# A mixture-of-experts stage computed on each token's two chosen experts, with rows sorted by expert through DRAM

## What is computed

```python
def _L1_ffn_ref(x, Wr, Wg, Wu, Wd):
    probs = jax.nn.softmax(x @ Wr, axis=-1)
    topk_w, topk_idx = jax.lax.top_k(probs, K)          # K = 2, E = 8
    topk_w = topk_w / jnp.sum(topk_w, axis=-1, keepdims=True)
    output = jnp.zeros_like(x)
    for i in range(E):
        sel = topk_idx == i
        w_i = jnp.sum(topk_w * sel.astype(x.dtype), axis=-1, keepdims=True)
        h = jax.nn.silu(x @ Wg[i]) * (x @ Wu[i])        # 256 x 256 each
        e_out = h @ Wd[i]
        output = output + w_i * e_out
    return output
...
    x = x + _L1_ffn_ref(_layernorm(x, axis=-1), L1_ffn_Wr, L1_ffn_Wg, L1_ffn_Wu, L1_ffn_Wd)
```

## Time and profile before

| | us |
|---|---|
| three runs | 3267.83, 3267.85, 3267.93 |
| median | 3267.85 |
| span of the profiled execution, first to last instruction | 3263.3 |
| median less span | 4.55 |
| of the span: expert stage, 2553.8 to 3263.3 | 709.5 |

### The profile page before, as it was taken

One profiled execution on the slowest core, in us unless ns is written; L12 is line 12 of the kernel. 1 busy time (PEld: TensorE's weight loads), 2 busy tenths in 40 slices (PEclk: granted clock), 3 DMA queues, 4 the chain that ended last, 5 costly groups with the idle time before them and its releaser, 6 DMA issues. The chain is left out here.

```text
span 3263.3 us, 78862 instructions
## 1 busy us (share of the span) xinstructions
PE 2803.0 (86%) x26196; PEld 1987.6 (61%) x26196; DVE 2373.2 (73%) x6843; ACT 1129.7 (35%) x2570; POOL 916.8 (28%) x1406
## 2 busy tenths in 40 slices
PE   3545549999999659998888849999999999999999
PEld 2433325555555359996666624444444799999999
DVE  6999967777777766666999947787777455555555
ACT  1222224555555422222333315565555211111111
POOL 3444432222222246664444422222222000000000
PEclk8676669999999879999999959999999999999999
DMA  3000033444444100000000044444444000000000
GB/s 88 0 0 0 0 97 84 87 86 86 86 86 85 24 1 0 0 0 1 0 0 0 0 128 92 94 87 94 94 85 84 5 5 6 6 6 5 6 6 7
DMA packets 230889, 132.42 MB, mean 41 GB/s; under 512 B 31328, under 2 KB 230400, under 8 KB 230816
## 3 DMA queue, kind: packets, MB, share of 16 engines
q1 hardware_dynamic: 226016, 127.05, 18.6%
...
## 5 line engine op out<-in xcount | busy, mean ns | idle before, releaser
L723 ACT ACTIVATE xattn_pr<-ps 128x384 f32<-128x384 f32 (+1 forms) x1024 | 536.6, 543 | 506.4 <-PE ps L493 233.3
L597 DVE TENSOR_REDUCE xattn_mx<-ps 128x2 f32<-128x512 f32 x512 | 342.0, 679 | 138.9 <-PE ps L459 128.7
L472 PE MATMUL ps<-xattn_qp,xattn_kp 128*128 128x192 bf16 (+1 forms) x2048 | 416.0, 264 | 3.0 <-DMA xattn_qp<-xattn_mrow 2.7
L459 PE MATMUL ps<-xattn_kp,xattn_qp 96*128 96x192 bf16 (+1 forms) x2048 | 372.5, 264 | 47.9 <-DMA xattn_kp<-xattn_rows 42.3
L593 DVE CUSTOM_DVE_ANT_0 xattn_masked<-ps,xattn_band 128x192 bf16<-128x192 f32 x1024 | 323.9, 353 | 106.9 <-issue 46.5
L472 PEld LDWEIGHTS ps<-xattn_qp,xattn_kp 128*128 128x128 bf16 x2048 | 163.9, 98 | 283.4 <-ACT xattn_pr L723 143.5
L1057 DVE SCALAR_TENSOR_TENSOR moe_tg<-moe_tanh,ps 128x256 f32<-128x256 f32 x256 | 107.8, 421 | 287.4 <-ACT moe_tanh L1027 287.4
L493 PE MATMUL ps<-xattn_pr,xattn_vs 128*32 128x256 f32 (+1 forms) x4096 | 303.3, 368 | 0.0
L493 PE MATMUL ps<-xattn_pr,xattn_ones 128*32 128x256 f32 (+1 forms) x4096 | 303.2, 368 | 0.0
L1027 ACT ACTIVATE moe_tanh<-ps 128x256 f32<-128x256 f32 x256 | 98.1, 383 | 587.1 <-PE ps L956 587.1
L956 PE MATMUL ps<-moe_xt,expert_g 128*128 128x128 f32 x2048 | 274.4, 277 | 0.0
...
## 6 DMA issues: line engine op xcount, KB each, us to landing
xattn_rows<-xattn_parts SPq DMA_DIRECT2D x128, 192.0 KB, 2.1
xattn_qp<-xattn_rows SPq DMA_DIRECT2D x256, 96.0 KB, 3.2
xattn_kp<-xattn_rows SPq DMA_DIRECT2D x256, 96.0 KB, 3.7
xattn_rows<-xattn_parts SPq DMA_DIRECT2D x128, 128.0 KB, 2.1
xattn_rows<-xattn_parts SPq DMA_DIRECT2D x128, 64.0 KB, 1.8
...
xattn_ctx<-in_ctx SPq DMA_DIRECT2D x32, 128.0 KB, 3.9
```

Of the source, the lines that this page charges most:

```text
L459: mm = nc.tensor.matmul(ps[:, BANK_S + j % RING, mt * D:mt * D + width], qp[u][s][0:R_MAX, h, mt * P:(mt + 1) * P], kp[u][s][0:R_MAX, h, l ...
L472: mm = nc.tensor.matmul(out, kp[u][s][:, h, nt * P:(nt + 1) * P], qp[u][s][:, h, lo:lo + width], start=True, stop=not banded)
L597: ins = nc.vector.tensor_reduce(mx[s][:, h * NT:(h + 1) * NT], ps[:, BANK_S + j % RING, :].rearrange("p (m n) -> p m n", m=NT), AX.X, ALU.max)
L723: nc.scalar.activation(out, src, ACT.Exp, scale=HD ** -0.5).then_inc(exped, 1)
```

## The change

The expert stage `gated_mlp(... moe ...)` is replaced by `routed_experts`, and its loops are written out.

- **Routing first.** All 32 pairs are normalised into `xn`, transposed and multiplied by the router. The steps of the softmax and of the ranks are done for groups of eight pairs (`G = 8`), four groups. PE counts, by products with a triangular matrix and with ones (`places`, `count`), which place each token has among those of its expert; DVE makes from it the row of each token in a table sorted by expert (`choices`, `block_table`), one table for each half of the tokens (`PARTS_R = 2`, 16 pairs each). Each expert's rows begin on a multiple of 128, so a half has 39 blocks of 128 rows at most, `BLOCKS = 2 * 2048 / 128 + 7`, and 39 are computed always.
- **Rows sorted through DRAM.** POOL scatters the normalised rows by indirect transfers, one per pair and choice: 32 per half, each of 128 rows of 1 KB. Rows of the table that no token uses stay zero from `clear_regions`, a new block of ten stores by SP at the start of the RWKV stage.
- **Blocks.** For each of the 78 blocks SP loads the rows (`load_block`, four buffers), PE transposes them, multiplies them by gate and up of the block's one expert in one product of 512 columns per weight tile (now the rows are the stationary side), transposes the hidden rows and multiplies by down. The number of the expert is read from SBUF into a register of PE (`expert_of`), and the weights are addressed by it. ACT copies both transposes out of PSUM and takes the tanh; DVE makes the hidden rows and copies the result to SBUF, SP stores it to DRAM.
- **Rows brought back.** POOL gathers for each pair the rows of both choices (`gather`, 64 in all, three buffers for each choice), DVE adds them by weight to `core.x` (`add_up`), SP stores. The sums of the first half are laid between the blocks of the second, those of the second half follow its last block.

The diff, cut to the parts that the working below speaks of:

```diff
--- before.py
+++ after.py
+PARTS_R = 2
+REGION = SEQS * T // PARTS_R
+BLOCKS = 2 * REGION // P + E8 - 1
...
-    g, u, d = (core.sb(f"expert_{n}", [P, NT, E8, D], ctx=ctx) for n in "gud")
+    gu = core.sb("expert_gu", [P, NT, E8, 2 * D], ctx=ctx)
+    down = core.sb("expert_d", [P, NT, E8, D], ctx=ctx)
...
+    each = 8
+    zero = core.sb("region_zero", [P, each, D], ctx=ctx)
+    made, cleared = nc.alloc_semaphore(name="region_zero_made"), nc.alloc_semaphore(name="region_cleared")
+    starts = range(0, ROWS, P * each)
+            nc.gpsimd.memset(zero[:].rearrange("p a d -> p (a d)"), 0.0).then_inc(made, 1)
+        @block.sync
+        def _(sp):
+            sp.wait_ge(made, 1)
+            for x in x_in:
+                for at in starts:
+                    n = min(each, (ROWS - at) // P)
+                    to = x[at:at + n * P, :].rearrange("(p a) d -> p a d", a=n)
+                    sp.dma_start(to, zero[:, 0:n, :]).then_inc(cleared, 16)
...
+        def sums_after(part, b):
+            if part == 0:
+                return []
+            return range(PP * b // BLOCKS, PP * (b + 1) // BLOCKS)
...
+                def load_block(part, b):
+                    n = idx(part, b)
+                    if b == 0:
+                        sp.wait_ge(scattered[part], 2 * 16 * PP)
+                    wait(sp, xb_turned, n - RB + 1)
+                    sp.dma_start(xb[n % RB][:], x_in[part][b * P:(b + 1) * P, :]).then_inc(xb_in[n % RB], 16)
+                def store_block(part, b):
+                    n = idx(part, b)
+                    sp.wait_ge(y_kept, n + 1)
+                    sp.dma_start(y_out[part][b * P:(b + 1) * P, :], yb[n % RB][:]).then_inc(yb_left[n % RB], 16)
+                def store_out(p):
+                    sp.wait_ge(summed, 2 * (p + 1))
+                    sp.dma_start(out_dram.rearrange("(n s) t d -> n (s t) d", s=S2)[p], acc[p % 2][:]).then_inc(left[p % 2], 16)
+                for b in range(RB - 1):
+                    load_block(0, b)
+                for n, (part, b) in enumerate(blocks()):
+                    if n + RB - 1 < PARTS_R * BLOCKS:
+                        load_block(*divmod(n + RB - 1, BLOCKS))
+                    store_block(part, b)
+                    for p in sums_after(part, b):
+                        store_out(p)
+                for p in range(PAIRS - PP, PAIRS):
+                    store_out(p)
...
+                def places(g):
+                    pe.wait_ge(routed, ROUTED * g + 11)
+                    wait(pe, routed, ROUTED * g)
+                    if g % PER == 0:
+                        wait(pe, tabled, TABLE * (g // PER - 1) + 1)
+                    flat = lambda q: sel[:, q, :, :].rearrange("p i e -> p (i e)")
+                    nc.tensor.matmul(ps[:, BANK_P, 0:G * E8], c[:, C_BEFORE:C_BEFORE + P], flat(g), start=True, stop=False)
+                    ones = c[:, C_ONES:C_ONES + P]
+                    for q in range(g // PER * PER, g):
+                        for i in range(G):
+                            nc.tensor.matmul(ps[:, BANK_P, 0:G * E8].rearrange("p (i e) -> p i e", e=E8), ones,
+                                             sel[:, q, i:i + 1, :].broadcast_to([P, G, E8]), start=False, stop=False)
+                    for i in range(G - 1):
+                        mm = nc.tensor.matmul(ps[:, BANK_P, (i + 1) * E8:G * E8].rearrange("p (i e) -> p i e", e=E8), ones,
+                                              sel[:, g, i:i + 1, :].broadcast_to([P, G - 1 - i, E8]), start=False, stop=(i == G - 2))
+                    mm.then_inc(placed, 1)
+                def count(part):
+                    last = (part + 1) * PER - 1
+                    pe.wait_ge(routed, ROUTED * (last + 1))
+                    n = 0
+                    for q in range(part * PER, last + 1):
+                        for i in range(G):
+                            n += 1
+                            mm = nc.tensor.matmul(ps[:, BANK_P, 0:E8], c[:, C_ONES:C_ONES + P], sel[:, q, i, :], start=(n == 1), stop=(n == PP))
+                    mm.then_inc(counted, 1)
...
+                def gate_up(part, b, e):
+                    n = idx(part, b)
+                    pe.wait_ge(xb_kept, n + 1)
+                    wait(pe, hidden, 2 * (n - 1))
+                    for kt in range(NT):
+                        mm = nc.tensor.matmul(ps[:, BANK_G + n % 2, :], xbt[n % 2][:, kt, :], gu[:, kt, bass.ds(e, 1), :].rearrange("p a f -> p (a f)"),
+                                              start=(kt == 0), stop=(kt == NT - 1))
+                    mm.then_inc(gu_made, 1)
+                def expert_of(n):
+                    part, b = divmod(n, BLOCKS)
+                    if b == 0:
+                        pe.wait_ge(tabled, TABLE * part + 9)
+                    return pe.value_load(expert[part][0:1, b:b + 1], min_val=0, max_val=E8 - 1)
+                turn_x(0)
+                pe.wait_ge(*landed)
+                for p in range(PAIRS):
+                    if p + 1 < PAIRS:
+                        turn_x(p + 1)
+                    logit_product(p)
+                    if p % G == G - 1:
+                        places(p // G)
+                        if p // G % PER == PER - 1:
+                            count(p // G // PER)
+                N = PARTS_R * BLOCKS
+                e = {0: expert_of(0)}
+                turn_block(0, 0)
+                gate_up(0, 0, e[0])
+                e[1] = expert_of(1)
+                turn_block(0, 1)
+                for n in range(N):
+                    if n + 2 < N:
+                        e[n + 2] = expert_of(n + 2)
+                    if n + 1 < N:
+                        gate_up(*divmod(n + 1, BLOCKS), e[n + 1])
+                    turn_hidden(*divmod(n, BLOCKS))
+                    if n + 2 < N:
+                        turn_block(*divmod(n + 2, BLOCKS))
+                    down_product(*divmod(n, BLOCKS), e[n])
...
+                keep_block(0, 0)
+                tanh(0, 0)
+                keep_block(0, 1)
+                for n in range(N):
+                    if n + 1 < N:
+                        tanh(*divmod(n + 1, BLOCKS))
+                    keep_hidden(*divmod(n, BLOCKS))
+                    if n + 2 < N:
+                        keep_block(*divmod(n + 2, BLOCKS))
...
+                for p in range(G):
+                    normalise_x(p)
+                for g in range(GROUPS):
+                    for p in range((g + 1) * G, min((g + 2) * G, PAIRS)):
+                        normalise_x(p)
+                    probabilities(g)
+                    ranks(g)
+                    choices(g)
+                    if g % PER == PER - 1:
+                        block_table(g // PER)
+                N = PARTS_R * BLOCKS
+                make_hidden(0, 0)
+                for n, (part, b) in enumerate(blocks()):
+                    if n + 1 < N:
+                        make_hidden(*divmod(n + 1, BLOCKS))
+                    keep_y(part, b)
+                    for p in sums_after(part, b):
+                        add_up(p)
+                for p in range(PAIRS - PP, PAIRS):
+                    add_up(p)
...
+                def scatter(p):
+                    for k in range(2):
+                        g.indirect_dma_start(x_in[p // PP], bass.IndirectOffsetOnAxis(ap=at[k][:, p:p + 1], axis=0), xn[:, p, :], None,
+                                             ).then_inc(scattered[p // PP], 16)
+                def gather(p):
+                    r = p % RY
+                    if p % PP == 0:
+                        for q in range(RB):
+                            g.wait_ge(yb_left[q], 16 * uses((p // PP + 1) * BLOCKS, q, RB))
+                    for k, y in enumerate((y1, y2)):
+                        wait(g, summed, 2 * (p - RY) + k + 1)
+                        g.indirect_dma_start(y[r][:], None, y_out[p // PP], bass.IndirectOffsetOnAxis(ap=at[k][:, p:p + 1], axis=0),
+                                             ).then_inc(y_in[k][r], 16)
+                for part in range(PARTS_R):
+                    g.wait_ge(tabled, TABLE * (part + 1))
+                    for p in range(part * PP, (part + 1) * PP):
+                        scatter(p)
+                for p in range(PAIRS):
+                    gather(p)
...
-        time_mixing(core, "rwkv", rwkv, mu, decay[:], bonus)
+        with ExitStack() as stage:
+            regions, cleared = clear_regions(core, stage)
+            time_mixing(core, "rwkv", rwkv, mu, decay[:], bonus)
+            nc.sync.wait_ge(*cleared)
...
-            gated_mlp(core, "moe", E8, lambda j, kt, ft: g[:, kt, j, ft * P:(ft + 1) * P],
-                      lambda j, kt, ft: u[:, kt, j, ft * P:(ft + 1) * P], lambda j, ft: d[:, ft, j, :], r, out, landed)
+            routed_experts(core, "moe", experts, regions, out, landed)
```

297 lines of the change are left out of this document (291 added, 6 removed).

## The result

| | before | after |
|---|---|---|
| median of four runs, us | 3267.84 | 3060.64 (3058.24 to 3063.06) |
| ratio to before | | 0.9366, 95% interval 0.9353 to 0.9379 |
| profiled execution, its time and span | see ahead | 3063.06 and 3060.9 |
| start of the expert stage, us from the span's start | 2553.8 | 2552.5 |
| length of the stage | 709.5 | 508.4 |

The change gains 207.2 us; 265.8 were forecast. The time lies in the range, 58.6 us above the forecast. The gain is in the expert stage, as its length shows (201.1 us shorter); what the stages ahead of it lost and won nearly cancels. In the combined kernel, the last experiment, one execution of four took 7128.8 us, which nothing here explains: the median in the table counts it, the median of the other three is 2969.28, and the interval of the ratio is that of those three.

What follows compares the result with a forecast made beforehand. PE was taken to bound the expert stage of 709.5 us. Start 2553.8, insertion 8, head 96, blocks 289 and tail 51 gave 2997.8; with 4.55 between span and median, 3002 us, range 2925 to 3120.

Steps and rivals of the forecast that it cites:

- G, the price of an indirect transfer: POOL's time for one scatter or gather: 1.3 us, twice a plain transfer, bounded between 0.64 and 5.9.
- the tail: After the last block: second half's gathers, additions and last store, together 51 us, 30 at the cheapest transfer price.
- the slower rival: POOL waits for each indirect transfer to land; from 4.5 us each all 128 are exposed, 3361 us at 5.7; chance 0.04.
- the first rival: Indirect transfers on POOL cost 2 to 4 us, lengthening head and tail: 3048 to 3176 us; chance 0.14.
- The chain of a block: Each of 78 blocks: gate and up, draining, hops, ACT's tanh and copy, down; 3.60 us, 3.7 with register operation.
- its register term: On PE in each block: register operation before each waiting product 0.09 us; loading the expert's number nothing, hidden behind down.
- The head: Routing before the first block: 96 us (70 to 130), from 98 by POOL's scatters and 68 to 107 by PE.
- Second half's scatters are hidden: 32 scatters on POOL, 42 us, run beside 39 blocks of 144 us and cost nothing.
- The insertion: Clearing the table before the RWKV stage, with its barrier: fill 2 to 4 us, ten issues 5.1; 8 us (6 to 10).
- a register load that is exposed: In the blocks, loading the expert's number costs up to 0.8 us each: 3067 us; chance 0.14 shared with late block loads.
- The lock of DVE and POOL: In the head, first 32 scatters and DVE's routing exclude one another; first block 35 us later, 3037 us; chance 0.12.
- The low clock: PE's clock stays low through the blocks: 6.4 us a block, 211 us more, 3213 us; chance 0.04.

Runs made afterwards that it cites:

- the combined kernel: Changed kernel with second half's scatters spread, hidden transposes after down, register load moved before the remaining wait, clearing without stage boundary; 2971.37 us, ratio 0.9076 to 0.9113.
- e7_load_moved: Changed kernel with the register load of the expert's number moved from before gate and up to before down; 2989.22 us, ratio 0.9137 to 0.9167.
- the narrow scatters: Changed kernel with every scatter moving only the first 32 of a row's 256 numbers; 3000.60 us, ratio 0.9166 to 0.9202.

## Why the prediction came out as it did

The profiled execution took 3063.06 us against 3002: 61 us, point by point.

- **G, the price of an indirect transfer: right.** Forecast 1.3 us, measured 0.96 us busy and 1.27 apart for scatters, 0.95 and 1.25 for gathers. This carried most of the risk, and the tail with it: forecast 51, measured 50.8. POOL waits for no landing, so the slower rival falls; so does the first rival. The Trainium skill, "GPSIMD Engine Reference", "Performance pitfalls for Q7 kernels", has a cost for a kernel that reads each gather index by a command of its own (some 102 cycles), from which the estimate of 10.9 us for 128 indices was worked out; the trace doesn't bear it out for this instruction, which reads 128 indices and is done in 0.96 us.
- **The chain of a block: right, and its register term too small.** The chain was put at 3.60 and is 3.59 with fixed experts. What was mis-sized is "one register operation ahead of each waiting product costs about 0.09" together with a load at nothing: with the register the period is 3.83, so 0.24 in place of 0.09, and 0.13 over the forecast's 3.70, 10 us in 77 blocks. The load was taken as hidden beneath the down product; moving it beneath PE's wait for ACT won 0.15 of these, and the 0.08 that stays with the products is what was forecast for the register operations. The term that was wrong is the load's own nothing. The Trainium skill, "DMA: Bandwidth & Descriptors", "Latency and other measured facts", gives such a load a floor of about 600 ns. The trace agrees, a little below it: 0.56 us where nothing covers it.
- **The pipeline's first block: left out.** Multiplying 78 blocks by the period leaves out that the first takes 10.0 us from its transposes to its copy (2675.2 to 2685.2), 6 more than a period.
- **The head: right where there is no hole.** Forecast 96 (98 by POOL); measured 96.5 without scatters and 98.1 to 98.6 on the chip without holes. That it came out to 2 us is luck on POOL's road: the table was ready after 53.8 us (forecast 48), and from the first scatter to the first block it is 44.8 us without a hole (e7_load_moved) where 50 was forecast. In the profiled execution the first hole made 122.7 of it. The clock was 0.50 all through, even with PE busy in 41.86 of 53.80 us; I had expected to lie between the levels.
- **"Second half's scatters are hidden": the step that failed.** POOL's own time was indeed hidden, and so was DMA. But during such a run TensorE's signals come late: 30 us in the blocks, 26 in the head, by the kernel without scatters. No row of before has a run of transfers of POOL beside a chain of PE, so nothing bounded it, and I costed it at nothing because POOL itself had time to spare. The first half's gathers, spread over the second half's blocks by the additions that they wait for, cost nothing, as forecast.
- **The insertion: wrong in place, and given back.** Forecast 8, measured 15 at its place (38.51 to 53.47). The fill took 1.80 us, just under its 2 to 4; ten issues took 10.79, against 5.1 from four at 0.51. The second wide attention stage started 10.3 us later than before and ended 1.2 earlier. There PE waited 17.2 us for transfers of `xattn_rows` where it had waited 28.3. That this belongs to the change is not shown: from its first reduction to the expert stage it took 607.3 us in this profile, 601.5 to 603.3 in those of the twelve experiments, and 618.9 in the only profile of before. That thirteen profiles of the new kernels lie below the old one speaks for the change; the cause is open.

The whole sum: start 9.3 us earlier than forecast, head 26.7 over, blocks 45.9 over (hole 30, period 10, first block 6), tail 0.2 under, and 2.2 us between span and time instead of 4.55, 2.4 under: 60.7. So the miss is the two holes, 56 us, and 5 us of smaller terms that partly cancel. Without holes the code takes 3000.6 us (the narrow scatters on the chip of group 2), and that this is so near to 3002 is luck: the start is 17.9 us earlier than forecast, the blocks are 15.2 over, the head 2.3 over, and tail and what lies around the span are 2.6 under.

Of the other rivals, a register load that is exposed was the right one to name, at 3067, but it allowed 0.8 us a block, and 0.13 over the forecast came. The block loads are never waited for in the steady pace. The lock of DVE and POOL named the right place and a similar sum (35 us in the head) by a mechanism that isn't there: DVE's steps of 512 elements take 0.69 us beside a scatter (2612.74), as in the earlier trace rows, and the scatter beside them took 1.46 us once instead of 0.96. The low clock falls as a rival: it is 1.00 in the blocks behind the second hole, and in the blocks low only in that hole, where PE mostly waits, and at their beginning, behind a head at 0.50.
